# Transformer layer with top-1 MoE: the output projection moved into the FFN's block, O^T stored as high and low part, the last LayerNorm in two VectorE instructions a tile

## What is computed

```python
xn = layernorm(x)
# differential attention: 16 heads, width 64, per batch of 512 tokens, on xn
P  = softmax(Q1 K1^T * s) - lam * softmax(Q2 K2^T * s)
O  = P @ V                                # 16 heads x 64 = 1024 columns
Y  = concat(O) @ Wo + bo                  # 1024 -> 256
attn = 0.2 * (gamma * (Y - mean(Y)) * rsqrt(var(Y) + 1e-5) + beta)
# FFN: each token goes to the one of 8 experts with the largest router probability
ffn = prob_max * (gelu(xn @ w1[e] + b1[e]) @ w2[e] + b2[e])
out = x + attn + ffn
```

## Time and profile before

| | us |
|---|---|
| median of three runs | 2054.06 (2049.75 to 2055.78) |
| the profiled execution, its own time | 2053.49 |
| its span, first to last instruction | 2051.5 |
| TensorE busy | 1903.1 (93% of the span) |
| VectorE busy | 1609.2 (78%) |
| ScalarE busy | 1493.6 (73%) |
| POOL busy | 909.5 (44%) |
| DMA, mean over the span | 205 GB/s |

### The profile page before, as it was taken

One profiled execution on the slowest core, in us unless ns is written; L12 is line 12 of the kernel. 1 busy time (PEld: TensorE's weight loads), 2 busy tenths in 40 slices (PEclk: granted clock), 3 DMA queues, 4 the chain that ended last, 5 costly groups with the idle time before them and its releaser, 6 DMA issues. The chain is left out here.

```text
span 2051.5 us, 39312 instructions
## 1 busy us (share of the span) xinstructions
PE 1903.1 (93%) x10625; PEld 1465.2 (71%) x10625; DVE 1609.2 (78%) x2960; ACT 1493.6 (73%) x3383; POOL 909.5 (44%) x893
## 2 busy tenths in 40 slices
PE   4369999999999999999999999999998699997885
PEld 4347767776777677767767776777675699997885
DVE  5448888888888888888888888888887456664566
ACT  3348888888888888888888888888887466665332
POOL 1234444444444444444444444444433365564676
PEclk9999999999999999999999999999999899999888
DMA  5778888788778777887888787777873866672564
GB/s 174 275 226 215 210 210 215 197 210 213 209 200 212 211 206 204 212 215 198 208 211 215 198 209 212 216 195 209 211 191 78 317 222 235 244 223 98 169 213 125
DMA packets 162207, 421.05 MB, mean 205 GB/s; under 512 B 27794, under 2 KB 69568, under 8 KB 146944
## 3 DMA queue, kind: packets, MB, share of 16 engines
q1 hardware_dynamic: 157408, 410.42, 70.7%
q0 software_dynamic: 4768, 10.25, 1.8%
HBM read 177.53 MB, written 41.72 MB: 107 GB/s over the span
## 5 line engine op out<-in xcount | busy, mean ns | idle before, releaser
L567 POOL TENSOR_TENSOR e<-e,rrec 128x512 f32<-128x512 f32 x512 | 532.1, 1039 | 832.1 <-DVE rrec L683 832.1
L644 ACT ACTIVATE e<-p_score,nmax 128x512 f32<-128x512 f32 x1024 | 695.2, 684 | 136.3 <-DVE nmax L708 135.5
L708 DVE TENSOR_REDUCE nmax<-p_score 128x2 f32<-128x1024 f32 x512 | 626.8, 1224 | 152.8 <-PE p_score L766 148.4
L766 PE MATMUL p_score<-ks,qs 128*128 128x512 f32 x2048 | 575.0, 402 | 6.6 <-ACT e L644 3.8
L754 PE MATMUL p_proj<-xp,w 128*128 (+1 forms) x1920 | 524.6, 409 | 21.2 <-SPq L482 21.2
L766 PEld LDWEIGHTS p_score<-ks,qs 128*128 128x128 f32 x2048 | 369.6, 188 | 180.6 <-ACT e L644 53.9
L754 PEld LDWEIGHTS p_proj<-xp,w 128*128 128x128 f32 x1920 | 339.8, 190 | 80.4 <-SPq L482 21.9
L694 DVE SCALAR_TENSOR_TENSOR pm<-e,coef 128x512 f32<-128x512 f32 x512 | 388.9, 760 | 0.0
L611 ACT COPY pT<-p_tr 128x512 f32<-128x512 f32 x512 | 301.3, 588 | 98.4 <-PE p_tr L776 97.8
L776 PE MATMUL p_tr<-consts,pm 128*128 128x128 f32 x2048 | 307.2, 273 | 2.3 <-ACT pT L611 2.3
L776 PEld LDWEIGHTS p_tr<-consts,pm 128*128 128x128 f32 x2048 | 254.6, 140 | 71.2 <-issue 2.5
(11 more groups left out here) (137 smaller groups left out, 1735.1 us busy)
## 6 DMA issues: line engine op xcount, KB each, us to landing
ks<-k_parts SPq DMA_DIRECT2D x512, 256.0 KB, 4.3
w<-weight_parts_scratch SPq DMA_DIRECT2D x64, 1280.0 KB, 8.1
qs<-q_parts SPq DMA_DIRECT2D x512, 128.0 KB, 2.9
w<-in_w SPq DMA_DIRECT2D x46, 1024.0 KB, 7.7
oT_scratch<-oT SPq DMA_DIRECT2D x64, 256.0 KB, 4.7
oTs<-oT_scratch SPq DMA_DIRECT2D x16, 1024.0 KB, 16.5
ys_scratch<-y SPq DMA_DIRECT2D x23, 256.0 KB
weight_parts_scratch<-n_wt_parts SPq DMA_DIRECT2D x4, 1280.0 KB, 7.3
```

Of the source, the lines that this page charges most:

```text
L567: nc.gpsimd.tensor_tensor(e1, e1, rrec[:, t % 4, 0:1].to_broadcast([P, S]), ALU.mult).then_inc(s_e1, 1)
L644: nc.scalar.activation(ex[:, t % 4, m, :], p_score[t % 2][:, m, :], ACT.Exp, bias=nmax[:, t % 2, m:m + 1], accum_out=rsum[:, t % 4, m:m + ...
L708: nc.vector.tensor_reduce(nmax[:, t % 2, :], p_score[t % 2][:, :, :], AXX, ALU.max, negate=True).then_inc(s_max, 1)
L766: last_op = nc.tensor.matmul(p_score[st % 2][:, m, :], qs[j][u][:, m, qt * P:(qt + 1) * P], ks[j][u][:, m, part, :], start=(part == 0), st ...
```

## The change

1. In attention, ScalarE's `copy_o` now writes the high part of O^T (fp32r), and a new VectorE instruction, `low_o`, subtracts it from the PSUM value: the low part. It stands in step 1 of each pair, after `combine`; for the last two pairs at the end. Both parts are stored (512 KB a pair), and `times_v` and `store_o` wait for the low part.
2. FFN and output projection are one block. The O^T parts are loaded straight into `op`, in three buffers that lie where FFN weights lay (`w1`, `w2`, the second `w1p`); each group is two DMAs of 1024 KB. The first is loaded once the last w1 has been split, the second once `hidden` of the last tile but one is done, the third once the last w2 has been split. `o_high` and `o_low` are gone. Two of the four PSUM banks are those of `p_x`.
3. The parts of Wo and bo are made during the FFN, after its third tile.
4. The statistics and `moments` stay. Then, per 128 tokens, `normed` computes (Y - mean) x gamma out of PSUM and `result` multiplies by 1/sigma and adds; what it adds is `base` = x + beta + prob x FFN row, computed between the reciprocal and the use of the root. ScalarE's L1259, POOL's L1227 and VectorE's L1302 and L1338 are gone. POOL still adds beta and gathers. The 16 groups are written out, not looped.

```diff
-        oT = [sb(f"oT{j}", [P, S]) for j in range(2)]
+        oT = [sb(f"oT{j}", [P, 2, S], F32R) for j in range(2)]
...
-                sp.wait_ge(s_o, pair + 1)
-                dst = oT_d[bass.ds(pair % PAIRS, 1), :, bass.ds(batch_of(pair) * S, S)]
-                sp.dma_start(dst.rearrange("a p n -> (a p) n"), oT[j][:, :]).then_inc(s_ost[j], 16)
+                sp.wait_ge(s_olo, pair + 1)
+                dst = oT_d[bass.ds(pair % PAIRS, 1), :, :, bass.ds(batch_of(pair) * S, S)]
+                sp.dma_start(dst.rearrange("a p c n -> (a p) c n"), oT[j][:, :, :].bitcast(F32)).then_inc(s_ost[j], 16)
...
-                nc.scalar.copy(oT[j][:, :], p_pv[:, :]).then_inc(s_o, 1)
+                nc.scalar.copy(oT[j][:, 0, :], p_pv[:, :]).then_inc(s_ohi, 1)
...
+            def low_o(pair, j):
+                dve.wait_ge(s_ohi, pair + 1)
+                nc.vector.tensor_tensor(oT[j][:, 1, :], p_pv[:, :], oT[j][:, 0, :].bitcast(F32), ALU.subtract
+                                        ).then_inc(s_olo, 1)
...
                     if st == 0:
                         copy_v(pair, j, first)
+                    if st == 1 and not first:
+                        low_o(pair - 2, j)
...
+            low_o(2 * ITERS - 2, 0)
+            low_o(2 * ITERS - 1, 1)
...
-                        pe.wait_ge(s_o, pair)
+                        pe.wait_ge(s_olo, pair)
...
+        def then(first, second):
+
+            with ExitStack() as early:
+                was = [early.enter_context(nc.sbuf_tensor(*x)) for x in first]
+            return was, [ctx.enter_context(nc.sbuf_tensor(*x)) for x in second]
+
+        w1, (op0,) = then([(f"w1_{j}", [P, KT, F], F32) for j in range(2)], [("op0", o_shape, F32R)])
+        w2, (op2,) = then([(f"w2_{j}", [P, FT, E], F32) for j in range(2)], [("op2", o_shape, F32R)])
+        w1p = [sb("w1p_0", [P, 2, KT, F], F32R)]
+        (w1p_1,), (op1,) = then([("w1p_1", [P, 2, KT, F], F32R)], [("op1", o_shape, F32R)])
+        w1p.append(w1p_1)
+        op = [op0, op1, op2]
...
+        (h,), acc = then([("h", [P, HG, 2, FFN_TILE], F32)], [(f"acc{r}", [P, 2, E], F32) for r in range(R)])
...
+        p_o = p_x + [ps(f"p_o{a}", [P, 2, E]) for a in range(2)]
...
+            def load_x(n):
+                if n >= R:
+                    sp.wait_ge(s_out, 2 * (n - R) + 2)
+                sp.dma_start(x[n % R][:, :, :], x_v[n]).then_inc(s_x[n % R], 16)
+
+            def load_o(n):
+                for c in range(2):
+                    sp.dma_start(op[n % OPS][:, c, :, :].bitcast(F32), oT_v[:, c, :, n * G:(n + 1) * G]
+                                 ).then_inc(s_op[n % OPS], 16)
+
+            for n in range(R):
+                load_x(n)
+
+            def first_o():
+                sp.wait_ge(s_w1lo, KT * FFN_TILES)
+                load_o(0)
+                sp.wait_ge(s_h, HG * (FFN_TILES - 1))
+                load_o(1)
+
+            turns(body, before_last=first_o)(sp)
+            sp.wait_ge(s_w2lo, FFN_TILES)
+            load_o(2)
...
+            for n in range(GROUPS):
+                if n + OPS < GROUPS:
+                    sp.wait_ge(s_oy, n + 1)
+                    load_o(n + OPS)
+                if n >= 2:
+                    store_out(n - 2)
+                    if n - 2 + R < GROUPS:
+                        load_x(n - 2 + R)
...
+            pool.wait_ge(s_scaled, 1)
+            for n in range(R):
+                add_beta(n)
+            pool.wait_ge(s_st[0], 16 * (LOOPED // 2 + 1))
+            pool.wait_ge(s_st[1], 16 * (LOOPED // 2))
+            for n in range(GROUPS):
+                fetch(n)
+                if n >= R:
+                    add_beta(n)
...
+            def output_weights():
+                nc.scalar.copy(wop[:, 0, :, :], wo[:, :, :]).then_inc(s_wohi, 1)
...
+            turns(body, after_third=output_weights)(act)
+            nc.scalar.activation(warm[:, :], consts[:, 0:4], ACT.Sqrt)
+            for q in range(GROUPS // 2):
+                act.wait_ge(s_d, MOMENT_STEPS * q + RECIPROCAL_STEP)
+                nc.scalar.activation(mom[q % 2][:, 5, :], mom[q % 2][:, 4, :], ACT.Sqrt).then_inc(s_root, 1)
...
+            def base(n):
+                r = n % R
+                dve.wait_ge(s_ff[r], 32 * (n // R + 1))
+                dve.wait_ge(s_xb, n + 1)
+                for s in range(2):
+                    v.scalar_tensor_tensor(out=x[r][:, s, :], in0=ff[r][s][:, :],
+                                           scalar=prob[:, 2 * n + s:2 * n + s + 1], in1=x[r][:, s, :],
+                                           op0=ALU.mult, op1=ALU.add).then_inc(s_base, 1)
+            def normed(n):
+                r, m = n % R, mom[n // 2 % 2]
+                if n >= R:
+                    dve.wait_ge(s_ost[r], 16 * (n // R))
+                for s in range(2):
+                    k = 2 * (n % 2) + s
+                    v.scalar_tensor_tensor(out=acc[r][:, s, :], in0=p_o[r][:, s, :], scalar=m[:, 0, k:k + 1],
+                                           in1=gamma, op0=ALU.subtract, op1=ALU.mult).then_inc(s_t, 1)
+            def result(n):
+                r, m = n % R, mom[n // 2 % 2]
+                dve.wait_ge(s_t, 2 * n + 2)
+                dve.wait_ge(s_base, 2 * n + 2)
+                for s in range(2):
+                    k = 2 * (n % 2) + s
+                    v.scalar_tensor_tensor(out=acc[r][:, s, :], in0=acc[r][:, s, :], scalar=m[:, 1, k:k + 1],
+                                           in1=x[r][:, s, :], op0=ALU.mult, op1=ALU.add).then_inc(s_out, 1)
+            for q in range(GROUPS // 2):
+                a = q % 2
+                done = [0]
+                def step(ins_):
+                    done[0] += 1
+                    ins_.then_inc(s_d, 1)
+                    dve.wait_ge(s_d, MOMENT_STEPS * q + done[0])
+                    if done[0] == RECIPROCAL_STEP:
+                        base(2 * q)
+                        base(2 * q + 1)
+                for c in range(2):
+                    n = 2 * q + c
+                    dve.wait_ge(s_oy, n + 1)
+                    for s in range(2):
+                        last_op = v.bn_stats(ostats[a][:, 2 * c + s, :], p_o[n % R][:, s, :])
+                    last_op.then_inc(s_bn, 1)
+                dve.wait_ge(s_bn, 2 * q + 2)
+                moments(nc, dve, step, ostats[a], mom[a], s_root, q + 1)
+                for c in range(2):
+                    normed(2 * q + c)
+                for c in range(2):
+                    result(2 * q + c)
...
+            pe.wait_ge(s_wohi, 3)
+            pe.wait_ge(s_wolo, 2)
+            for n in range(GROUPS):
+                c, r = n % OPS, n % R
+                pe.wait_ge(s_op[c], 32 * (n // OPS + 1))
                 if n >= R:
+                    pe.wait_ge(s_t, 2 * (n - R) + 2)
...
-    oT_d = nc.dram_tensor("oT_scratch", [PAIRS, P, T], F32).ap()
+    oT_d = nc.dram_tensor("oT_scratch", [PAIRS, P, 2, T], F32).ap()
```

More of the change, by code:

```diff
@@ L957, in _ @@
+            store_out(GROUPS - 2)
+            store_out(GROUPS - 1)
+            for r in range(R):
+                sp.wait_ge(s_ost[r], 16 * (GROUPS // R))
             sp.wait_ge(s_st[0], 16 * (LOOPED // 2 + 1))
@@ L1215, in fetch @@
-                if n == 0:
-                    pool.wait_ge(s_scaled, 2)
-                pool.wait_ge(s_x[r], 16 * (n // R + 1))
-                nc.gpsimd.tensor_tensor(x[r][:, :, :], x[r][:, :, :], wide(beta), ALU.add).then_inc(s_xb, 1)
-            fetch(0)
-            fetch(1)
-            for n in range(GROUPS):
-                if n + 2 < GROUPS:
-                    fetch(n + 2)
-                r = n % R
-                pool.wait_ge(s_norm, n + 1)
-                nc.gpsimd.tensor_tensor(yn[r][:, :, :], yn[r][:, :, :], wide(gamma), ALU.mult).then_inc(s_gamma, 1)
@@ L1264, in _ @@
-        @block.tensor
-        def _(pe):
-            pe.wait_ge(s_lo, 2)
-            def body(i, first, last):
-                for r in range(R):
-                    n, c = R * i + r, r % 2
-                    pe.wait_ge(s_olo, n + 1)
-                    if not first:
-                        pe.wait_ge(s_norm, n - R + 1)
-                    for s in range(2):
-                        for part in range(2):
-                            nc.tensor.matmul(p_y[r][:, s, :], ones_r[:, :], bop[:, part, :],
-                                             start=(part == 0), stop=False)
-                        for k in range(PAIRS):
-                            for t, (e, f) in enumerate(((0, 0), (0, 1), (1, 0))):
-                                last_op = nc.tensor.matmul(
-                                    p_y[r][:, s, :], op[c][:, e, k, s * P:(s + 1) * P], wop[:, f, k, :],
-                                    start=False, stop=(k == PAIRS - 1 and t == 2))
-                    last_op.then_inc(s_y, 1)
-            looped(pe, TURNS, body)
@@ new lines, in _ @@
+                    for part in range(2):
```

(15 more changed lines are left out.)

235 lines of the change are left out of this document (62 added, 173 removed).

## The result

| | before | changed |
|---|---|---|
| median of the runs, us | 2054.31 (2049.75 to 2055.78, 4 runs) | 2017.45 (2016.13 to 2019.53, 4 runs) |
| the profiled execution, us | 2053.49 | 2017.64 |
| its span, us | 2051.5 | 2015.7 |
| TensorE busy | 1903.1 us (93%) | 1891.1 us (94%) |
| VectorE busy | 1609.2 us (78%) | 1615.7 us (80%) |

The ratio is 0.9825, with a 95% interval of 0.9808 to 0.9843: 36.9 us less; the forecast was 2020.5.

What follows compares the result with a forecast made beforehand. TensorE set attention's pace; a four-engine wait loop slowed the output stage. Output stage -30.6, tail -7.4, attention +2, its end +2.1, FFN +0.6: -33.3 from 2053.49, so 2020.2; median forecast 2020.5 us, range 2011 to 2038.

Steps and rivals of the forecast that it cites:

- Output stage, TensorE: Output stage: 146.0 us become 115.4, from 111.4 of matmuls at full clock plus 4 for DMA; -30.6.
- The DMA's charge of 4 us: Output stage: the last O^T lands near 1996 where TensorE wants it at 1991.8; bounds 0 and 21 us.
- the 367: Output stage: DMA rate in GB/s assumed for O^T loads, between the trace's fullest stretches of 353 to 372.
- Tail: After the last matmul: 18.1 us become 10.7 with the new normalization, -7.4.
- Attention: Attention pairs: `low_o` takes 0.68 of 0.73 us slack before the projection of v, +2 us; attention's end, +2.1.
- the upper bound of 42.3: Attention pairs: the whole added instruction would be paid in every pair, 62 x 0.683 us.
- (c): Attention rival: VectorE's lateness reaches TensorE in part of the pairs, 19 us instead of 2, 2037.5 us; chance 0.13.
- (d): Attention rival: `low_o` makes TensorE wait at the projection of v in every pair, 42.3 us, 2060.8 us; chance 0.04.
- FFN: FFN: splitting Wo and bo on VectorE between tiles 2 and 3 costs +0.6 us; bounds 0 and 3.4.
- Loop of waits: Output stage before: `o_low` stands behind `combine`, which waits for POOL and that for ScalarE; 11.1 us of waits inside.
- (a): Output stage and attention rival: the DMA never binds and attention loses nothing, 2014.5 us; chance 0.2.
- (b): Output stage rival: the DMA becomes the bound at 314 GB/s, delay 21 instead of 4 us, 2037.5 us; chance 0.12.

Runs made afterwards that it cites:

- run 7: The change with a fourth buffer for O^T, over the space of an FFN weight tile free by then: 2014.97 us.
- run 4: The change with a third, unread O^T load of 1024 KB per group from the fourth group on: 2050.67 us.
- Run 3: The change without VectorE's low part of O^T; the low half is zero, stored and multiplied as before: 2015.01 us.
- runs 1 and 2: The change with VectorE's low-part subtraction done twice in step 1 of each pair, 2042.51 us; with the second subtraction in step 7 instead, 2017.49 us.
- experiment 5: Also Run 5: the kernel before, with the low part of an output tile computed ahead of the previous tile's combination on VectorE: 2055.87 us.
- two edits: On the change: a fourth buffer for O^T, 2014.97 us; the last W2's low part on VectorE instead of GpSimd, 2014.01 us; both together 2018.32 us.
- run 9: The change with both a fourth O^T buffer and the last W2's low part on VectorE: 2018.32 us.
- run 11: The version with fourth O^T buffer and last W2's low part on VectorE, its fourth O^T load moved behind the first output tile: 2017.64 us.
- run 6: The kernel before with only the new normalization in its output stage; O^T conversion and the hole stay: 2029.78 us.

## Why the prediction was right, and where not

The forecast was 2020.5 us, the result 2017.45: right in direction, mechanism and size, 3 us too high. (Its own sum, 2020.2 and 0.6 for the median, is 2020.8.)

*Output stage, TensorE.* Forecast 115.4 us (111.4 and 4), measured 113.5. The floor was mis-sized by 0.9: run 7 shows 110.5, as a half group takes 3.45 us now and took 3.48. The DMA's charge of 4 us came out at 3.0. The fourth load did start when group 0 ended, as forecast, and from there to the start of the last group (1898.5 to 1998.2) the DMA moved 373 GB/s on average, close to the 367 that I took from the earlier trace rows. But it did not move them evenly: 155, 343 and 351 GB/s in the first three stretches of 4 us, then 383 on average from 1910 to 1998. At 387 throughout, 37.0 MB take 95.6 us; with 1 us more the last O^T would land at 1995.1, as early as TensorE can want it (1891.6 + 15 x 6.9 = 1995.1). So by this estimate the 3.0 us are the slow start. Run 7 does not remove it (262 to 365 GB/s from 1898 to 1922); its fourth group loaded ahead covers it. That my even rate came out so close is in part luck, since I had seen neither the slow start nor the higher steady rate. The waits under 1 us cost no clock, as forecast.
The figure of the Trainium skill ("DMA: Bandwidth & Descriptors", Specifications), some 358 GB/s for a core, is exceeded by this case, a program on one core: 383 GB/s as the mean of 88 us of the change (1910 to 1998), 386 of 78 us in run 4.

*Tail.* Forecast 10.7, measured 10.6, each term within 0.3 us: `normed` and `result` took 3.2 where 3.5 was said, the store and the end 2.8 where 2.6 was.

*Attention.* Forecast: 2 us for the pairs, 2.1 for the end. Run 3 gives 2.4 us for all low parts together, and it still stores both parts, for which 0.7 was forecast. The profiles agree: TensorE's first matmul of the FFN's start (the table of tokens) comes 5.0 us later in the change (1594.13 and 1599.17), of which 1.4 are there before attention begins (the same matmul of norm and routing starts at 24.09 and 25.51) and have nothing to do with the change. So 3.1 to 3.6 where 4.1 was said, and nothing of the upper bound of 42.3. The argument (the instruction fits into the 0.73 us ahead of the projection of v and reaches nobody) is shown by the slack of 0.14 that is left and by runs 1 and 2: one more instruction there costs 25 us, the same in step 7 nothing. Rivals (c) and (d) had their mechanism right and the point from which it decides too: it begins just beyond what the change adds. By the Trainium skill ("SBUF — State Buffer", SBUF: two separate sides) an instruction with an input in PSUM stays out of the lock between VectorE and GpSimd; the trace agrees, though not by L683: it took 0.68 us every time, but in none of its 64 places did a GpSimd instruction on data run beside it. The low part L670, with its data input in PSUM, took 0.74 us in the 25 cases between 400 and 1500 us in which the splitting (L552) ran beside it, as in all others; `combine` took 1.01 in the 24 cases beside L554 and 0.74 otherwise.

*FFN.* Forecast +0.6. In the change the last `hidden` starts at 1872.03, before at 1866.02, +6.0, of which 5.0 were there at the FFN's start; the rest, up to 1.0, is what the FFN added, small as forecast. Not foreseen: in the two profiles the outputs of the last tile took 7.43 us before and 5.72 in the change, both behind the same wait of 2.64 us for W2. I took it first for a gain. It is none: the change run again took 7.42, and in experiment 5, with the code of before, it was 5.73. Of ten profiles with this wait, eight show 7.3 to 7.5 and two 5.7. The comparison of the two spans holds 1.7 us of luck, the medians need not. The FFN's end, 4.2 us later where 4.7 was forecast, is thus closer than its parts: 1.4 us of later start and 1.7 of shorter last outputs nearly cancel in it, and neither belongs to the change.

*Loop of waits.* The prediction said that `o_low` stands behind `combine`, which waits for GpSimd and ScalarE. That was half of it. Run 5 took `o_low` from behind `combine` and gained nothing: `o_high` stands behind the same normalization on ScalarE. The forecast did not suffer, since the change removes both.

*Rivals.* (a), no DMA cost and no attention cost, 2014.5: run 7 reaches its number (2014.97) with a fourth buffer, but only its first condition, since attention costs there what it costs in the change. (b) is what run 4 shows: it needs 1 MB more a group. The change itself stands close to that edge: 2.88 MB in 6.9 us want 417 GB/s, 387 are to be had, and the buffers loaded ahead pay for most of the difference, over only 16 groups.

## What to carry to other kernels

Ask of an added instruction not how idle its engine is but who waits behind the place where it stands: the same 0.68 us in each pair cost 25 us in step 1 and nothing in step 7. Where a stage waits in a loop through three engines, moving an instruction on one of them only changes the name in the wait; take the other engines out of the loop. And before you join two edits that each gain, look at what they do together: each of these two brought some 3 us, which is not far above the scatter of the runs, both together none.

## What the runs showed of the hardware

- The DMA of one core moved 383 GB/s of mostly 1 KB runs over 88 us (the change) and 386 over 78 us (run 4); in the kernel before I had only seen bursts of 372.
- TensorE can stand still in the middle of a group without waiting for anything that the profile shows: 2.8 us in run 9, 1.5 in run 11, 0.2 in one profile of the change, always early in the output stage. Behind the first two it also lost clock (5.49 and 5.13 us for the next 24 matmuls).
- VectorE's two additions L1307, both inputs in SBUF, took 0.88 us before and 3.10 at 1947.67 in run 5, where GpSimd's two tensor instructions (1947.55 to 1950.1) ran beside them. Instructions with their data in PSUM did not show this: the row maximum L713 took 1.22 to 1.23 us beside GpSimd's L567 in 338 cases of attention in the change, and as long in the 49 without.
- The same wait of 2.64 us was followed by slow clock in eight of ten profiles and not in two. A single profile can't say what such a wait costs. In the output stages, TensorE's waits of up to 1.28 us never slowed the 24 matmuls behind them (2.99 to 3.14 us); of those of 1.4 to 3.5 us nearly all did (4.35 to 5.49 us), but one of 1.48 in run 6 and one of 1.68 in run 4 did not.
- SP takes long to issue when many loads are in flight. In the change a group's first load of O^T took it 0.37 us at 1919.16, the second 2.28 and the output's store 2.65 at 1915.17; in the kernel before, each of these issues took 0.4. So late in the stage SP issued loads up to 3.9 us after their buffer was free (TensorE was done with it at 1974.9, the load came at 1978.74). The DMA still moved 377 GB/s from 1974 to 1986, so this cost little if anything; no run tests it.
